# A five-layer graph network on one core: layer 0 with four steps behind its strips in place of seven, and the GRU ahead of each group's sum in them

## The reference

```python
h = relu(enc(relu(layernorm(x))))            # two products with 128x128 weights
for w in conv_w:                             # 5 layers
    agg = segment_sum((h @ w)[src], dst, num_segments=12500)
    gi = agg @ gru_wih.T + gru_bih           # three gates of 128
    gh = h @ gru_whh.T + gru_bhh
    r, z = sigmoid(ir + hr), sigmoid(iz + hz)
    n = tanh(i_n + r * h_n)
    h = (1 - z) * n + z * h
out = x + sigmoid(dec(relu(h)))
```

## Time and profile before

| | us |
|---|---|
| median of 3 runs | 5796.78 (5784.28 to 5811.27) |
| profiled execution, its time | 5798.54 |
| its span | 5796.8 |
| TensorE matmuls busy | 4920.1 (85%) |
| ScalarE busy | 3837.8 (66%) |
| GpSimd busy | 3455.7 (60%) |
| VectorE busy | 2130.5 (37%) |

### The profile page before, as it was taken

The page is one execution under the profiler, slowest core; times in us unless marked ns, Lnnn a source line. Parts: engine busy times, 40 slices in busy tenths (PEclk is TensorE's granted clock), DMA queues, the critical chain, the costliest instruction groups (busy, mean ns, idle before and its releaser), DMA issues.

```text
span 5796.8 us, 65249 instructions
## 1 busy us (share of the span) xinstructions
PE 4920.1 (85%) x21744; PEld 3635.7 (63%) x21744; DVE 2130.5 (37%) x5021; ACT 3837.8 (66%) x3047; POOL 3455.7 (60%) x3554
## 2 busy tenths in 40 slices
PE   5368888888789999977998988798989878999897
PEld 3256666666566666756666766566666656766674
DVE  7466666767322222231222222222222222222223
ACT  5267777777567676755766666576767646767674
POOL 3555556555466666646666666566666656666654
PEclk7689999999899999988999998899999989999998
DMA  6787878778756666676666667666666766666664
GB/s 203 230 237 233 235 233 246 228 234 259 252 182 206 197 203 209 204 240 200 197 196 209 206 197 252 186 198 198 205 201 200 236 216 185 191 193 197 184 189 123
DMA packets 711002, 1215.98 MB, mean 210 GB/s; under 512 B 282849, under 2 KB 441570, under 8 KB 710562
## 3 DMA queue, kind: packets, MB, share of 16 engines
q1 hardware_dynamic: 540992, 748.04, 42.3%
q0 software_dynamic: 169264, 462.12, 26.0%
q10 hardware_dynamic: 434, 1.81, 0.1%
HBM read 1015.23 MB, written 196.41 MB: 209 GB/s over the span
## 4 chain that ended last, share of the span: by engine, by line
PE 65%; ACT 11%; issue 9%; another core or an unknown queue 9%; DVE 4%; DMA 1%; SPq 0%; DVEq 0%; POOL 0%; ACTq 0%; POOLq 0%
PE strip_ps L1936 31%; PE four_ps L1936 14%; ACT counts L1134 8%; PE agg_ps L1812 3%; PE four_ps L1812 2%; PE four_ps L1922 2%; ACT room L1109 2%; PE r_ps L1828 2%; PE z_ps L1828 2%; PE r_ps L1834 1%; PE z_ps L1834 1%; PE four_ps L1835 1%; PE r_ps L1858 1%; PE four_ps L1754 1%
## 5 line engine op out<-in xcount | busy, mean ns | idle before, releaser
L948 POOL DMA_INDIRECT messages<-table,src_stage x3503 | 3408.5, 973 | 2229.2 <-issue 1025.6
L1134 ACT ACTIVATE counts<-raw 128x2048 fp32r<-128x2048 uint8 x1382 | 2285.7, 1692 | 918.9 <-remote 391.2
L1936 PE MATMUL strip_ps<-counts,parts 128*128 128x512 f32 x9212 | 2467.0, 420 | 240.6 <-issue 111.9
L1936 PEld LDWEIGHTS strip_ps<-counts,parts 128*128 128x128 f32 x9212 | 1779.2, 197 | 798.7 <-issue 291.2
L1936 PE MATMUL four_ps<-counts,parts 128*128 128x512 f32 x4116 | 1048.3, 408 | 104.1 <-issue 63.8
L1134 ACT ACTIVATE counts<-third_raw 128x2048 fp32r<-128x2048 uint8 (+1 forms) x522 | 861.0, 1689 | 403.6 <-remote 201.4
L1936 PEld LDWEIGHTS four_ps<-counts,parts 128*128 128x128 f32 x4116 | 786.1, 194 | 337.7 <-issue 122.7
L1418 DVE TENSOR_TENSOR selection<-agg_ps,dst_stage 128x1024 fp32r<-128x1024 bf16 (+1 forms) x269 | 327.5, 1218 | 1182.7 <-remote 703.5
L1418 DVE TENSOR_TENSOR selection<-four_ps,dst_stage 128x1024 fp32r<-128x1024 bf16 (+1 forms) x172 | 207.8, 1208 | 952.6 <-remote 496.0
L1109 ACT ACTIVATE room<-four_ps 128x784 uint16<-128x784 f32 x448 | 363.6, 822 | 155.9 <-remote 93.9
L1812 PE MATMUL agg_ps<-messages,selection 128*128 128x256 f32 x2147 | 344.5, 302 | 51.3 <-issue 34.8
(11 more groups left out here) (232 smaller groups left out, 3694.3 us busy)
## 6 DMA issues: line engine op xcount, KB each, us to landing
raw<-adjacency SPq DMA_DIRECT2D x691, 448.0 KB
third_raw<-adjacency SPq DMA_DIRECT2D x261, 448.0 KB
adjacency<-room SPq DMA_DIRECT2D x112, 784.0 KB
parts<-table SPq DMA_DIRECT2D x35, 1792.0 KB
messages<-table,src_stage POOLq DMA_INDIRECT x3503
table<-table_stage SPq DMA_DIRECT2D x108, 512.0 KB
h_old<-states SPq DMA_DIRECT2D x120, 256.0 KB
states<-h_new SPq DMA_DIRECT2D x108, 256.0 KB
```

What stands on the lines that cost most here:

```text
L948: nc.gpsimd.indirect_dma_start(messages[:, slot, t, :, :].rearrange("p i f -> p (i f)").bitcast(F32), None, table[k.layer % 2], bass.Indir ...
L1134: nc.scalar.activation(to, raw_piece[:, :, a * EIGHTH:e * EIGHTH].rearrange("p q (k d) -> p k q d", d=EIGHTH), ACT.Copy).then_inc(expanded, 1)
L1936: last = mm(strip_banks[k.bank_of(i)], parts[:, block, half, :], counts[:, 0 if k.first else p % 2, at, :], start=(p == 0 and at == 0 and ...
```

## The change

Layer 0 gets a light-step count of its own, `FIRST_LIGHT = 4`, so that the same units and sets are spread over steps up to 95. Layer 1's four early pieces come two in a step, in steps 96 and 97. Chunk 11's phase 1 is in step 96 and chunk 23's in step 97; chunk 11 has phases 1 and 2 in one step and 3 and 4 in the next, and chunk 23 has 2 and 3 in one. In the light steps the GRU's work stands in front of the group's sum on TensorE and in front of `combine` on VectorE. The products of chunk 24 that need only its old state are issued in step 99.

```diff
-AHEAD, FRONT, LIGHT = 4, 12, 7
+AHEAD, FRONT, LIGHT, FIRST_LIGHT = 4, 12, 7, 4
...
-        self.end = self.steps - LIGHT
+        self.end = self.steps - (FIRST_LIGHT if self.first else LIGHT)
...
-            return self.n_pieces + (0 if self.layer == LAYERS - 1 else min(AHEAD, step + 1 - self.end))
+            return self.n_pieces + (0 if self.layer == LAYERS - 1 else min(AHEAD, (2 if self.first else 1) * (step + 1 - self.end)))
...
+        own = (self.dense - 1, LAST - 1) if self.first else ()
         for step, chunk in sorted(ready) + [(self.steps, LAST)]:
-            at = self.gru_at[chunk] = max(step, at + 3)
+            if chunk not in own:
+                at = self.gru_at[chunk] = max(step, at + 3)
+        if self.first:
...
+            self.gru_at[self.dense - 1], self.gru_at[LAST - 1] = self.end, self.end + 1
...
         t = step - self.gru_at[chunk] + 1
-        if self.first or chunk != LAST - 1 or step < self.steps - 2:
+        if self.first and chunk == self.dense - 1 and t >= 1:
+            return [1, 2] if t == 1 else [3, 4] if t == 2 else [t + 2]
+        if chunk != LAST - 1 or step < self.steps - 2:
             return [t]
...
-                if step == k.gru_at[k.dense - 1] + 5:
+                if step == (k.steps - 1 if k.first else k.gru_at[k.dense - 1] + 5):
                     for portion in late:
                         next_portion(k, portion)
...
+                    if step >= k.end:
+                        gru_steps(step, 2, 3, 4)
                     combine(k, c, s)
...
+                    if step >= k.end:
+                        gru_steps(step, "table")
+                        gru_steps(step, "old update", "sum update", "old reset", "sum reset")
+                        gru_steps(step, "sum candidate", "old candidate")
+                    if step == k.steps - 1:
+                        n = k.order.index(LAST)
+                        old_update(n, LAST_J, h_old[n % 2], (h_loaded[n % 2], 16 * (n // 2 + 1)))
+                        old_reset(n, LAST_J, h_old[n % 2])
                     sum_group(k, c, s)
```

## The result

Over 20 runs each, the changed kernel took 5819.99 us (median; 5771.88 to 5858.16) against 5795.7 us (5775.44 to 5813.75) before: ratio 1.0046, 95% interval [1.0029, 1.0064]. It is slower by about 0.46%, just inside my bound for "same", and above my range. The profiled execution of the changed kernel took 5799.18 us (span 5797.4 us), 21 us under the median, so it is read for where time moved, not for the total.

The account below looks back on a forecast made before the run. In the strips four resources, TensorE busiest at 86%, are near full and wait for each other; behind them a chain sets the time. -8.4 + 6 = -2.4 us on 5796.8 gives 5794 us, range 5778 to 5812 us.

Parts of the forecast that it names:

- my bound for "same": Whole kernel: a change within about 0.5%, 29 us, cannot be told from none; chance of same 0.86.
- The light stretch: Layer 0 behind the last strip's work, up to layer 1's first large matmul run: 65.4 to 57 us, saving 8.4.
- The three added steps in the strips: Layer 0's strips: three more groups cost 6 us, between 3.9 by TensorE's time and 13 by transfers.
- Rival 2: Layer 0's strips: each step keeps its 13.73 us, three more cost 41 us, kernel 5830 us; chance 0.06.
- Rival 1: Contention for transfers eats or reverses the gain: +13 us in strips, -8 in light stretch, 5802 us; chance 0.2.
- Rival 3: Chunk 23's table lands late behind both portions, layer 1 starts at 60 in place of 57 us, 5797 us; chance 0.15.

Follow-up runs that it names:

- cut: Kernel before and changed kernel, each with layers 1 to 4 left out: 1327.72 and 1344.51 us, run again 1331.4 and 1345.23 us.
- c_after: Changed kernel with layers 1 to 4 left out: 1344.51 us, against 1327.72 us for the kernel before with the same left out.
- c_after_even: Changed kernel without layers 1 to 4, layer 0's units given out in whole pieces: 1586.74 us on a slower chip, no base beside it.
- c_after_fs12: Changed kernel without layers 1 to 4, first strip in step 12 in place of 9: 1576.5 us on a slower chip, no base beside it.
- c_before: Kernel before with layers 1 to 4 left out, the base for the cut runs: 1327.72 us.
- c_before_g4: Kernel before without layers 1 to 4, only four of eight gathers issued in 88 of layer 0's 101 groups: 1351.05 us on the 5905 us chip.
- c_before_pe: Kernel before without layers 1 to 4, each group's eight matmuls issued twice: 1576.66 us on the 5905 us chip, no base beside it.

## Why the prediction was wrong

*The light stretch* was right in its sum. I had -8.4 us. To layer 1's first large run, which is what I had reckoned, it is -7.3 (65.4 to 58.1); to chunk 24's transposes -8.1 on the chip of the profile and -7.3 and -7.7 cut. The order of the chain was as laid out, but not its waits. Chunk 22's copy was not held (it ran 0.8 us behind T0, where I had 3.4), and "old reset" of chunk 11, which I had waiting some 3 us for it, shows no wait. In their place ScalarE's units for layer 1 waited 4.21 us and were released by a store of counts (`adjacency<-room`), and its copy for chunk 11 came 2.7 us behind the start of its transposes (1522.44 - 1519.74), held by a table's transfer. The errors cancel, and that is luck: 58.1 us where I had 57.

*The three added steps in the strips* is the term that failed. I took 6 us, between TensorE's 3.9 and the transfers' 13. It is 22.5 us in the trace of the whole kernel, 24.7 and 25.6 cut. Both bounds priced what a group does, on the busiest resource, and took it that all else of a step is only moved. The step sums above say what came instead, in the cut kernels. A unit taken out of a step does give back its time, some 2 us. But a full step of 11.6 us less four such units leaves 3 to 4 us that come again with each added step (an estimate from the table, for a unit together with the little else that goes with it), 9 to 12 us for three; this alone is above my 6 and near my upper bound. The other 13 to 16 us lie in the full steps that begin in the middle of a piece, which the change makes by spreading 336 units over 87 steps, and for which the sum has no term. The group's own matmuls and VectorE work are a small part of these 3 to 4 us: doubled or added to in the kernel before, they cost a third of their length and almost nothing. A strip step by the prediction's own measure, from turned group to turned group, is 13.52 us, (1494.5 - 399.3)/81, where I had 13.3 and before 13.73.

*Rival 2*, "paced as a step", with 41 us and a chance of 0.06, is nearest in size but not in its reason: the steps are not of fixed length, since those with three units are 2 us shorter. The mean step shrinks by 0.12 us only (11.61 to 11.49) because short steps and longer ones are averaged. I had dismissed the rival on GpSimd's being ahead, which says only that the gathers are not the pace.

*Rival 1*, contention, carries a part: with half of each piece's bytes the change costs 5 to 8 us less. It is the loads of the pieces; halving the gathers took nothing off it (25.8 us in the strips).

*Rival 3*, the late table, happened in small. The transfer of chunk 23's table is what ended ScalarE's wait, and the copy starts 1.53 us behind the start of its transposes (1555.29 - 1553.76), against 0.72 before (1547.30 - 1546.58): 0.8 us, where I had 3. The Trainium skill ("DMA: Bandwidth & Descriptors", "Queues, rings and completion order") says that descriptors of a ring are consumed in order. The trace of c_after agrees in direction: the table issued behind the two portions took 12.0 us from issue to landing, where the median of the 36 tables of this size is 6.1 (first fence from 1318 to 1342 us, second the whole trace):

```profile
parts<-table SPq DMA_DIRECT2D x2, 1792.0 KB, 10.4
table<-table_stage SPq DMA_DIRECT2D x1, 512.0 KB, 12.0
```

```profile
table<-table_stage SPq DMA_DIRECT2D x36, 512.0 KB, 6.1
```

*What stays open.* Why a full step from mid-piece is longer, and whether whole pieces in every step would take this time back. The traces show the form: TensorE idle 16.2 us more, ScalarE waiting for TensorE's units 70 times in place of 47, while ScalarE's own work did not grow (887 and 890 us). That the broken pieces set the two engines out of step was the last theory, and the two kernels that were to test it (c_after_even, c_after_fs12) fell on a slower chip, without a base beside them. It is supported by the lengths of the steps and not shown by an experiment. The place of the turned group (up to 5 to 7 us) and the loads of the pieces (some 10, 24.7 - 15.2) overlap with it and do not add up. At the level of the result, where TensorE is busy longer at a lower clock and steps from mid-piece are hardly longer, the split of the 22.5 us is open.

## What to carry to other kernels

When work is spread over more steps, do not price an added step by what its own group executes. Take a full step, subtract what the work that is moved gives back, and count the rest once for each added step: here 11.6 us less four units of some 2 us, 3 to 4 us. Then look at how the work divides: spreading units that come in pairs over a number of steps that they do not fill evenly made 42 steps begin in the middle of a piece, and in these traces such steps were longer. A stretch with little work may be the cheap place for fixed steps: moving three of them saved 7 to 8 us there and cost 25 us among full ones. And a resource that is early (the gathers) is excluded as the pace only itself; it excludes no other step-wise pace. No changed version that was run beside its base beat the kernel before.

## What the runs showed of the hardware that I had not expected

The same kernel stands at different levels on different chips: before took 4887, 5796 and 5905 us. ScalarE's copy of a unit is as long at either level (1.70 us in the profile before, 1.71 us in c_before), and so is a turned group at its median (0.270 us). Two things differ in the strips, 1149.9 against 975.0 us: TensorE is idle for 165 us in place of 45, and it is busy for 985 us in place of 930, at a mean granted clock of 0.95 in place of 1.00. So 120 of the 175 us are waits; the other 55 are the same matmuls at the lower mean clock.

On the 5905 us chip the kernel before, cut, took 1351.05 us with half of the gathers left out (c_before_g4), and 1576.66 us, 1546.62 at the lowest, with all gathers and each group's matmuls twice (c_before_pe). The doubled matmuls cost 31 us on a quicker chip, so by this estimate some 165 to 195 us went with the gathers, although GpSimd waited for TensorE's buffers in both. The strips were 966.2 us with half of the gathers, as on a quick chip with all (975.0), and 1178.4 us in c_before_pe. No pair on that chip differs in the gathers alone, so I take it as likely, not as shown, that on such a chip the gathers slow down engines that do not wait for them; by what way, no run here shows.
